# A split bias row in place of zero products, a finer first weight load, and two jobs moved to VectorE

## The reference, cut to what matters

```python
# x: (64, 128, 1024), cond: (64, 512), W3: (512, 1024), W2: (1024, 1024)
q_emb = relu(cond @ W3 + b3)                       # (64, 1024)
v_sum = sum(x, axis=1, keepdims=True)
y = (128 * x + v_sum) * q_emb[:, None, :]
out = x + relu(y @ W2 + b2)
```

## Time and profile before

| | |
|---|---|
| median of 3 runs | 636.22 us (636.18 to 636.4) |
| the profiled execution's own time | 635.75 us |
| its span in the trace | 634.0 us |
| granted TensorE clock over the span | 1.00 |
| PE busy | 629.2 us (99%) |
| DVE busy | 444.1 us (70%) |
| ACT busy | 418.9 us (66%) |
| POOL busy | 16.5 us (3%) |
| DMA moved | 108.83 MB |

### The profile page before, as it was taken

How to read it: one execution, slowest core, us unless ns; L and a number is a source line. 1 busy time by engine, 2 the same in 40 slices (tenths; PEclk the granted TensorE clock), 3 DMA queues, 4 the chain that set the end, 5 groups by cost and what they waited for, 6 DMA issues and landing times.

```text
span 634.0 us, 9260 instructions
## 1 busy us (share of the span) xinstructions
PE 629.2 (99%) x2795; PEld 518.4 (82%) x2796; DVE 444.1 (70%) x675; ACT 418.9 (66%) x897; POOL 16.5 (3%) x21
## 2 busy tenths in 40 slices
PE   9999999999999999999999999999999999999997
PEld 6888888888888888888888888888888888888886
DVE  3989979576776757677576776757677576776533
ACT  4879886839577594856839577494866839577320
POOL 2340000000000000000000000000000000000000
PEclk9999999999999999999999999999999999999999
DMA  8935736454353734436353353733346353350703
GB/s 301 400 138 196 264 136 227 173 197 143 141 182 132 256 141 135 137 158 232 132 199 137 139 187 132 255 142 131 134 165 232 132 199 132 144 189 0 259 6 132
DMA packets 26656, 108.83 MB, mean 172 GB/s; under 512 B 2961, under 2 KB 3089, under 8 KB 22802
## 3 DMA queue, kind: packets, MB, share of 16 engines
q1 hardware_dynamic: 26496, 108.54, 47.9%
q10 hardware_dynamic: 146, 0.14, 0.1%
HBM read 75.11 MB, written 33.55 MB: 171 GB/s over the span
## 4 chain that ended last, share of the span: by engine, by line
PE 92%; DVE 2%; issue 0%; POOL 0%; ACT 0%; DVEq 0%
PE acc L285 92%; DVE vsum L597 1%; DVE w_lo L678 1%; DVE scale L603 0%; DVE a_lo L662 0%; POOL x_sb L572 0%; DVE xn L686 0%; ACT a_hi L386 0%; DVE bias L605 0%; DVEq L691 0%
## 5 line engine op out<-in xcount | busy, mean ns | idle before, releaser
L285 PE MATMUL acc<-w_hi,a_hi 128*128 128x512 f32 x904 | 352.2, 390 | 0.2
L285 PE MATMUL acc<-w_lo,a_hi 128*128 128x512 f32 x904 | 351.7, 389 | 0.0
L285 PE MATMUL acc<-w_hi,a_lo 128*128 128x512 f32 x904 | 351.7, 389 | 0.0
L404 ACT ACTIVATE x_sb<-x_sb,bias,scale 128x128 f32<-128x128 f32 x492 | 203.2, 486 | 9.6 <-DVE bias L605 9.5
L285 PEld LDWEIGHTS acc<-w_hi,a_hi 128*128 128x128 f32 x904 | 169.7, 188 | 36.7 <-DVE a_lo L662 1.0
L285 PEld LDWEIGHTS acc<-w_hi,a_lo 128*128 128x128 f32 x904 | 169.7, 188 | 35.4
L285 PEld LDWEIGHTS acc<-w_lo,a_hi 128*128 128x128 f32 x904 | 169.7, 188 | 35.0
L673 DVE TENSOR_TENSOR a_lo<-x_sb,a_hi 128x512 fp32r<-128x512 f32 x150 | 103.5, 690 | 106.9 <-ACT a_hi L399 106.2
L399 ACT CAST a_hi<-x_sb 128x512 fp32r<-128x512 f32 x150 | 93.3, 622 | 39.5 <-PE acc L285 38.1
L399 ACT CAST a_hi<-s 128x512 fp32r<-128x512 f32 x60 | 37.4, 623 | 74.0 <-PE acc L285 69.1
L597 DVE TENSOR_REDUCE vsum<-x_sb 128x16 f32<-128x2048 f32 (+1 forms) x38 | 73.7, 1943 | 6.9 <-DMA x_sb<-x_t 6.7
(11 more groups left out here) (49 smaller groups left out, 192.9 us busy)
## 6 DMA issues: line engine op xcount, KB each, us to landing
xn<-x SPq DMA_DIRECT2D x64, 512.0 KB, 4.0
out<-xn SPq DMA_DIRECT2D x62, 512.0 KB, 3.2
x_sb<-x_t SPq DMA_DIRECT2D x30, 1024.0 KB, 5.1
x_sb<-w_t SPq DMA_DIRECT2D x4, 512.0 KB, 6.1
x_sb<-x_t SPq DMA_DIRECT2D x8, 256.0 KB, 11.7
u_sb<-w_q SPq DMA_DIRECT2D x3, 512.0 KB, 8.0
m_sb<-w_q SPq DMA_DIRECT2D x3, 512.0 KB, 7.6
w_stage<-w_q SPq DMA_DIRECT2D x2, 512.0 KB, 9.0
```

Source lines behind the costliest of these rows:

```text
L285: return nc.tensor.matmul(dst, lhs, rhs, start=False, stop=False, skip_group_check=True)
L404: last = nc.scalar.activation(x_sb[:, slot, t, k], x_sb[:, slot, t, k], ACT.Identity, bias=bias[:, slot, t, k:k + 1], scale=scale[:, slot, ...
```

## The change

- The six zero products between the q sums and the float32 product with the row of ones go. In their place the half row of b2 is split as the other operands are: ScalarE copies the ones and the row to fp32r (`row_ones`, `row_hi`), VectorE makes `row_lo`, and TensorE adds both parts to banks 3, 2 and 4 by six products of one row by 512 columns (`b_row_part`). Banks 2 and 4 are then no longer seeded by ScalarE.
- The first half of B11 is loaded by two DMAs of 256 KB (`load_b11`), the second of them after W3 part 3; quarter 2 is loaded ahead of the second half of B11, and `b_first` behind quarters 3 and 4.
- Sums 6 and 7 for q move from before k-step 2 of plain product 0 to before its k-step 1. On ScalarE `q_relu(6)` and `q_relu(7)` move ahead of the casts of B11's pieces 2 and 3.
- On VectorE the low parts of B11's pieces 2 and 3 go behind the sums and scalars of quarter 2, `scale_first(3)` goes ahead of `low_first(2)`, quarter 7 is scaled there (`scale_first(7)`, before on GpSimd), `low_first(6)` stands before both sums for `t1`, and b_step is formed there, between `scalars_usual` and the low parts of B22, the second of which goes behind `low_first(8)`.
- `seed_r` of the first pair stands two steps earlier on ScalarE.
- The last result is made and stored in four parts of 128 columns, stored in turn by SP and by ScalarE's DMA queue.

```diff
+    ROWS = (3, 2, 4)
+    SEEDED = (5, 6, 7, 0, 1)
-    SEEDED = (2, 4, 5, 6, 7, 0, 1)
...
+        row_hi = a_hi[0:1, 6].rearrange("p k n -> p (k n)")
+        row_lo = a_lo[0:1, 6].rearrange("p k n -> p (k n)")
+        row_ones = a_hi[0:1, 3, 0]
...
+            def load_b11(k):
+                sp.dma_start(w_stage[:, k], w2_q[0, 0, :, k * MH:(k + 1) * MH]).then_inc(b11_first[k], 16)
...
             load_w3(2)
-            load_half(w_halves, 0, 0, 0, b11_loaded)
+            load_b11(0)
             load_w3(3)
+            load_b11(1)
+            load_first(2)
             load_half(w_halves, 0, 0, 1, b11_loaded)
-            load_first(2)
-            load_b(b_first, 0, b_first_loaded)
             for n in (3, 4):
                 load_first(n)
+            load_b(b_first, 0, b_first_loaded)
...
+            for n in (0, 2):
+                part = slice(n * MH // 4, (n + 1) * MH // 4)
+                sp.wait_ge(part_done, n + 1)
+                sp.dma_start(out[2 * (2 * p + 1) + 1, :, part], xn[:, 1, 1, part]).then_inc(tail_stored, 16)
...
-            def keep_warm(n):
-                for _ in range(n):
-                    last = add(acc[:, 2], warm[:, :P], warm[:])
-                return last
+            def b_row_part(n, part):
+                return add(acc[:, ROWS[n]], row_ones, part)
...
             for k in range(KT - 2):
                 q_sum(k)
-                if k == KH - 1:
-                    pe.wait_ge(ones_set, 1)
-                    pe.wait_ge(row_loaded, 16)
-                    add(acc[:, 3], ones[:], b_row)
-                last = keep_warm(1)
-            last.then_inc(marked, 1)
+                if k == 1:
+                    pe.wait_ge(row_hi_ready, 1)
+                    b_row_part(0, row_hi)
+                if k == 2:
+                    pe.wait_ge(row_lo_ready, 1)
+                    b_row_part(0, row_lo)
+                if k == 3:
+                    b_row_part(1, row_hi)
+                if k == 4:
+                    b_row_part(1, row_lo)
+                    b_row_part(2, row_hi)
+            b_row_part(2, row_lo).then_inc(marked, 1)
...
                     if n == 0 and k == 0:
                         pe.wait_ge(lo_started, 1)
-                    if n == 0 and k == KH // 2:
+                    if n == 0 and k == 1:
                         q_sum(KT - 2)
                         q_sum(KT - 1)
+                    if n == 0 and k == KH // 2:
                         pe.wait_ge(lo_ready, 1)
...
+            act.wait_ge(ones_set, 1)
+            nc.scalar.copy(row_ones, ones[:])
+            act.wait_ge(row_loaded, 16)
+            nc.scalar.copy(row_hi, b_row).then_inc(row_hi_ready, 1)
             act.wait_ge(small_loaded, 16)
             for k in range(KH):
                 q_relu(k)
             cast_first_half(0)
-            cast_w("b11", 0, b11_loaded[0], 16)
+            cast_w("b11", 0, b11_first[0], 16)
             cast_first_half(1)
-            cast_w("b11", 1, b11_loaded[0], 16)
             for k in (4, 5):
                 q_relu(k)
-            for k in range(2, W_PIECES):
-                cast_w("b11", k, b11_loaded[k // 2], 16)
-            cast_first(1)
+            cast_w("b11", 1, b11_first[1], 16)
             for k in (6, 7):
                 q_relu(k)
-            act.wait_ge(marked, 1)
-            act.wait_ge(b_first_loaded, 16)
-            seed_plain(2, b_first)
+            for k in range(2, W_PIECES):
+                cast_w("b11", k, b11_loaded[1], 16)
+            cast_first(1)
             scale_first(2)
             cast_first(2)
             act.wait_ge(q_ready, KT)
-            for bank in (4, 5):
-                seed_plain(bank, b_first)
+            act.wait_ge(marked, 1)
+            act.wait_ge(b_first_loaded, 16)
+            seed_plain(5, b_first)
...
+            for n in (1, 3):
+                part = slice(n * MH // 4, (n + 1) * MH // 4)
+                act.wait_ge(part_done, n + 1)
+                act.dma_start(out[B - 1, :, part], xn[:, 1, 1, part]).then_inc(last_stored, 16)
...
-            for n in (1, 4, 7):
+            for n in (1, 4):
                 scale_first(n)
...
-            pool.wait_ge(b_seeded, len(SEEDED))
-            nc.gpsimd.tensor_tensor(b_step[:], b_step[:], b_first[:], ALU.subtract).then_inc(b_step_ready, 1)
...
+            dve.wait_ge(row_hi_ready, 1)
+            nc.vector.tensor_tensor(row_lo, b_row, row_hi.bitcast(fp32), ALU.subtract).then_inc(row_lo_ready, 1)
...
-            for k in range(1, W_PIECES):
-                low_w("b11", k)
+            low_w("b11", 1)
             sums_0(2)
             scalars_0(2)
+            for k in range(2, W_PIECES):
+                low_w("b11", k)
             low_first(1)
             sums_0(3)
             scalars_0(3)
+            scale_first(3)
+            low_first(2)
             sums_0(4)
-            low_first(2)
             scalars_0(4)
-            scale_first(3)
+            low_first(3)
+            low_w("b21", 0)
             sums_0(5)
             scalars_0(5)
-            low_first(3)
-            low_w("b21", 0)
...
             scalars_0(7)
+            scale_first(7)
+            low_first(6)
...
+            dve.wait_ge(b_seeded, len(SEEDED))
+            nc.vector.tensor_tensor(b_step[:], b_step[:], b_first[:], ALU.subtract).then_inc(b_step_ready, 1)
+            low_w("b22", 0)
             low_first(8)
+            low_w("b22", 1)
...
-            for c in range(2):
-                c21(p, 1, c)
+            c21(p, 1, 0)
+            dve.wait_ge(prod_done, done_by(p, 4, 1))
+            for n in range(4):
+                part = slice(n * MH // 4, (n + 1) * MH // 4)
+                o = xn[:, 1, 1, part]
+                nc.vector.scalar_tensor_tensor(o, p_bank(1, 1)[:, part], 0.0, o, ALU.max, ALU.add).then_inc(part_done, 1)
```

More of the change, by code:

```diff
@@ L98, in cond_residual @@
         small_loaded, row_loaded, ones_set = sem("small_loaded"), sem("row_loaded"), sem("ones_set")
+        row_hi_ready, row_lo_ready = sem("row_hi_ready"), sem("row_lo_ready")
         b_first_loaded, b_step_loaded = sem("b_first_loaded"), sem("b_step_loaded")
@@ L102, in cond_residual @@
         x1_loaded = [sem(f"x1_loaded{c}") for c in range(2)]
+        b11_first = [sem(f"b11_first{k}") for k in range(2)]
         b11_loaded = [sem(f"b11_loaded{h}") for h in range(2)]
@@ L110, in cond_residual @@
         stored = [[sem(f"stored{c}{t}") for t in range(2)] for c in range(2)]
-        tail_stored = sem("tail_stored")
+        tail_stored, part_done, last_stored = sem("tail_stored"), sem("part_done"), sem("last_stored")
         table_set, warm_set = sem("table_set"), sem("warm_set")
@@ L271, in _ @@
                 sp.dma_start(out[2 * (2 * p + c)], xn[:, c, 0]).then_inc(stored[c][0], 16)
-            for r, h in ((c22_done, 1), (c21_done, 0)):
-                half = slice(h * MH, (h + 1) * MH)
-                for c in range(2):
-                    sp.wait_ge(r, 2 * p + c + 1)
-                    sp.dma_start(out[2 * (2 * p + c) + 1, :, half], xn[:, c, 1, half]).then_inc(tail_stored, 16)
+            for c in range(2):
+                sp.wait_ge(c22_done, 2 * p + c + 1)
+                sp.dma_start(out[2 * (2 * p + c) + 1, :, MH:], xn[:, c, 1, MH:]).then_inc(tail_stored, 16)
+            sp.wait_ge(c21_done, 2 * p + 1)
+            sp.dma_start(out[2 * (2 * p) + 1, :, :MH], xn[:, 0, 1, :MH]).then_inc(tail_stored, 16)
+            for n in (0, 2):
+                part = slice(n * MH // 4, (n + 1) * MH // 4)
+                sp.wait_ge(part_done, n + 1)
+                sp.dma_start(out[2 * (2 * p + 1) + 1, :, part], xn[:, 1, 1, part]).then_inc(tail_stored, 16)
             for c in range(2):
@@ L279, in _ @@
                 sp.wait_ge(stored[c][1], 16 * (PAIRS - 1))
-            sp.wait_ge(tail_stored, 64)
+            sp.wait_ge(tail_stored, 80)
+            sp.wait_ge(last_stored, 32)
         @block.tensor
@@ L304, in _ @@
                 nc.tensor.matmul(acc[:, n], warm[:, :P], warm[:], start=True, stop=True)
-            keep_warm(4)
+            for _ in range(4):
+                add(acc[:, 2], warm[:, :P], warm[:])
             pe.wait_ge(small_loaded, 16)
@@ L534, in pair @@
                         seed_p(p, parity, i - 2)
-                    if i in (5, 6):
+                    if first and i in (3, 4):
+                        seed_r(p, i - 3)
+                    if i in (5, 6) and not first:
                         seed_r(p, i - 5)
@@ L758, in _ @@
             scalars_0(7)
+            scale_first(7)
+            low_first(6)
             dve.wait_ge(w_lo_ready, split("b11", W_PIECES - 1))
-            dve.wait_ge(b12_loaded[0], 16)
-            w_sum(w_halves, v_halves, w_halves, 0, t1_ready)
-            low_first(6)
-            dve.wait_ge(b12_loaded[1], 16)
-            w_sum(w_halves, v_halves, w_halves, 1, t1_ready)
+            for h in range(2):
+                dve.wait_ge(b12_loaded[h], 16)
```

(7 more changed lines are left out.)

## The result

The changed kernel takes 642.78 us (median of 5 runs, 642.25 to 643.06) against 636.18 for the kernel before; the ratio is 1.0104 with a 95% interval of 1.0090 to 1.0119. It is 6.6 us slower, where no difference was forecast. The profiled execution is the one of 642.78 us, its span 641.0 us.

The account below looks back on a forecast made before the run. TensorE was taken as the bound, busy 99% of the span. Terms: +0.93 at k-step 2, -0.63 of gaps closed, -0.3 at the end, sum 0.0; median forecast 636.2 us, range 635.1 to 637.2.

Parts of the forecast that it names:

- the price of a one-row product: In the q sums: each fp32r row part costs between 0.07 and 0.23 us; 0.23 was taken.
- The bound "from above": For a row part in the q sums: at most the main run's rate, 0.23 us, same type and 512 columns.
- the clock falls: Rival, 6%: in the q sums or the stall before k-step 2, half rate for 3.5 us costs 1.7 us: 637.9.
- The first product: First plain product on TensorE begins at 12.9 us, 0.16 earlier than before.
- the one over W3 part 2 and the q sums: Ahead of the first plain product: W3 part 2 lands at 10.3, then sums 4, 5 and row parts end at 12.9.
- The one over B11's first piece: Ahead of the first plain product: piece lands at 10.95, low part starts at 12.06, TensorE could start at 12.87.
- The stall before k-step 2: In plain product 0: piece 2's cast waits behind q_relu(7); 1.18 us stall, k-step 2 at 17.35, 0.93 later than before.
- What comes back: After k-step 2: TensorE's three later waits on low parts of tokens vanish, giving back 0.63 us.
- All three gaps close: At products 2, 3 and 11: with slack 0.5 us no waits remain; product 11 begins at 45.93, +0.30.
- The end: Last result in four stored parts: gain 0.3 us, bounds a gain of 0.5 and a loss of 0.2.
- The two reasons that I had named as its bounds: At the last store: rows of 512 bytes or the second queue's issue eat the difference, a loss of 0.2 us.
- the forecast's own range: Whole kernel, the main forecast case with 68%: 636.2 us, within 635.7 to 636.7.

Follow-up runs that it names:

- full height: The changed kernel with its six one-row products made 128 rows high, rows 1 to 127 being zeros: 636.71 us against 636.20 for the kernel before, ratio 1.0005.
- zeros: The changed kernel with a 128-row bf16 zero product in place of each one-row product, b2's row left out: 635.93 us against 636.05 for the kernel before.
- 96 rows: The changed kernel with its six one-row products made 96 rows high, rows 1 to 95 being zeros: 636.36 us against 636.11 for the kernel before.
- Casting first: Changed kernel with 128-row products, casts and low parts of B11's pieces 2 and 3 and cast_first(1) moved ahead again: 635.95 us against 636.23 for the kernel before.

## Why the prediction was wrong, point by point

Two steps failed, and both are about the height of the six row products. The second is the larger.

- **The step that failed first: the price of a one-row product.** "From below it costs what a zero product does, 0.07, from above the rate of the main run, 0.23. I take 0.23." It measured 0.50 us (1.46 for a sum with one, less 0.955), outside both bounds, because the load behind it is not pulled ahead but stands idle for 0.24 us. At full height the same product measured 0.17, inside them. The bound "from above" came from rows of full height. The trace of before had the warning: behind the float32 product of one row the next load stands 0.76 us idle on "issue". I read that as the length of a slow product.
- **The step that failed by most: the clock, put at 6%.** The rival "the clock falls" was answered with "Against: six products of 512 columns remain" and priced at 1.7 us. It came true, and with a larger price: the clock was low for 13.6 us, not 3.5, through sums 5 to 7, the stall and the first products. Six products of 96 or 128 rows in these places do hold the clock: in three forms of the changed kernel (zeros, full height, 96 rows) and in the kernel before with only the row change, no run of 41 has a mean clock under 0.999. Six of one or 64 rows do not (four kernels, all 17 runs). The count was the wrong thing to look at. Whether it is the idle time beside such products or the low products themselves that let the clock fall is not shown.
- **How the 6.6 us divide.** Full height takes back 6.07. Beside the kernel with 96 rows, whose clock stays up, the changed kernel is 1.13 us late at the load behind sum 4 (12.17 against 11.04), before the clock falls. At k-step 2 it is 4.66 late (22.36 against 17.70), and the unbroken run takes 615.41 us in place of 613.62, 1.79 more: 6.45 in all, where the medians differ by 6.42. I put about 1 us of it on the changes of height and about 5.5 on the low clock. This is an estimate: it takes the rest of the q sums at the steps seen at full clock (the first product would begin at about 14.3, against 13.31 in the kernel with 96 rows, which waits 0.73 us there for a low part). With zero products beside the one-row ones the height costs more, 2.3 us (638.25 for the runs with a full clock, against 635.93), since idle time then stands on both sides of each and six products are added.
- **The first product.** Forecast 12.9; 15.70 in the changed kernel, 12.98 at full height. The number is right at full height, partly by luck. Of the two ways that led to it, the one over W3 part 2 and the q sums was 0.9 us too long: the last row part is loaded at 11.79, and the loads then stand idle for 1.00 us. The one over B11's first piece held (low part from 12.17, forecast 12.06), though the piece landed at 11.50 and not at 10.95.
- **The stall before k-step 2.** Forecast at 17.35 with 1.18 us of waiting; 17.38 at full height, with 1.39 us of idle loads. Casting first removed it and 0.76 us. Right, with the products priced rightly; in the changed kernel it came 5 us later.
- **What comes back.** "All three gaps close": from k-step 2 on the run has 2706 matmuls without a gap, also at full height, where k-step 2 stands where it was forecast. Right; when k-step 2 came earlier by casting first, a wait of 0.3 to 0.7 at product 1 took their place.
- **The end.** Forecast 0.3 us, measured 0.0 to 0.1 by the traces (3.14 to 3.22 against 3.23 us from the first read of the last result to the end), nothing by the medians. The term was mis-sized. The two reasons that I had named as its bounds are both seen, rows of 512 bytes at 0.7 of the rate and a slow issue on the second queue, and are not told apart.
- **The sum for everything but the shape** was 636.2; the full-height kernel gave 636.71, at the upper edge of the forecast's own range of 635.7 to 636.7, and the one with 96 rows 636.36.
